# The first batch's key rotation in tiles of its own, its parts stored one by one, and a new order of steps in a two-layer adaLN kernel

## The chip, the cores and the metric

The kernel runs on one core of a Trainium2 chip. The time is that of one execution on the device in microseconds, lower is better; the median of several executions is compared. TensorE (PE, with its weight loads PEld), VectorE (DVE), ScalarE (ACT), GpSimd (POOL) and the sync engine (SP, which here issues most of the DMAs) run side by side, each through its own instructions in order, and wait for each other on semaphores.

## What is computed

Two layers, each with an attention part and a feed-forward part, both modulated per batch by rows computed from a condition (sa, ca, ga for the first part, sb, cb, gb for the second). Eight batches of 512 tokens of 128 channels. The reference, cut:

```python
mod = (_silu(L0_c) @ L0_wmod).reshape(8, 6, 1, -1)
sa, ca, ga, sb, cb, gb = ...
h = _layernorm(x) * (1 + ca) + sa
x = x + ga * attn0(h)     # 16 heads of 8, rotary q and k, softmax without scale
h = _layernorm(x) * (1 + cb) + sb
x = x + gb * ffn0(h)      # 8 experts, hidden 256, silu(h w0) * (h w1) @ wo, best two of 8
mod = (_silu(L1_c) @ L1_wmod).reshape(8, 6, 1, -1)
h = _layernorm(x) * (1 + ca) + sa
x = x + ga * attn1(h)     # v, gate = silu(n W_hidden + b); q, k from silu(n W_qk + b);
                          # softmax of q^T k / 512 over channels, summed, scales v; times gate; W_out
h = _layernorm(x) * (1 + cb) + sb
x = x + gb * ffn1(h)      # batch b goes through expert b: gelu(h w1 + b1) w2 + b2
```

The rotation turns each pair of channels of q and k by an angle that grows with the token's place: rot(t) = t cos + t2 sin, with t2 the pair exchanged and one sign changed.

## The kernel before, in words

The work of one batch passes through four stages, and batches overlap: batch b is in one stage while b+1 is in the stage before.

- **P**: layer norm and modulation, transposition, products with the weights of q, k and v, rotation, and a split of q and k (float32) into three bf16 parts each. The parts are stored to a buffer in DRAM (`parts_d`) and loaded back as stacks `qs` and `ks` of 48 rows per head, in which one bf16 product of 48 rows sums the six products of parts that make a near-float32 score.
- **A**: four groups of four heads. For each group the scores are computed once for their row maxima (`smax`: PE product, DVE reduction into negmax, 16 one-bank units per group in the first two batches, `EARLY`), the maxima are split into parts by POOL (`mparts`), turned by PE (`mT`), taken to a row by ACT and by a DMA into the stacks as rows 48 to 50; then the scores are computed again transposed with the maximum already taken off (`sexp`), exponentiated by ACT and multiplied with v (`pv`).
- **B**: the first layer's experts. Tokens are scattered by expert to DRAM, gathered in tiles, and go through w0, w1 (units) and the down product. The last batch goes through all experts densely: its down products are `ldown(e)` (L1225), its sums on DVE are at L1932.
- **C**: the second layer. `up(c)` (L1339, names xdn and w1) and `dn` (L1361) are the products of its feed-forward part, `out` (L1311) that of its attention part, `upb` (L1324) a product of a row of ones with a bias row, in the last batch only. Between `up` and `dn` DVE and ACT compute the gelu: DVE's u at L2045 takes a bank that ACT has copied and frees it for the next `up`.

**What sets the order.** On each engine the steps stand in an order given by a table of numbers, `SLOTS`: for each step (stage, name, arguments, batch) its place on each engine. `walk` issues the steps of an engine in that order. An engine does nothing out of this order, so a step that waits holds everything behind it. PE, DVE, ACT, POOL and SP have 1277, 989, 706, 530 and 667 rows of instructions in it (adjacent equal ones taken together).

**The first batch.** Its q product and then its k product go to one bank, `m1`: the k product waits until q's rotation has read it. The rotation on DVE has three steps (L1755 cos, L1757 and L1759 the two halves of sin), into tiles `rot1` and `rot2`; `first_split` (L1715) adds them to `rem`, ACT rounds `rem` to the first part (L1484), `first_split2` (L1720) takes it off, ACT rounds the second (L1488), `first_split3` (L1725) takes it off, which is the third. Rotation and split of k use the same three tiles and wait for those of q. Later batches do the split on POOL. q's three parts are stored when the third is there (three DMAs of one step), k's likewise, and the stacks are loaded in four portions of two head pairs each, 16 DMAs. The modulation rows of both layers are finished by DVE at L1689 to L1703 in one block and stored to `mod_d`, from which later rows (ga, gb, crow, cgb) are loaded.

## Time and profile before

| | |
|---|---|
| median of 3 runs | 981.61 us (981.26 to 983.02) |
| the profiled execution | 982.85 us |
| its span in the trace | 981.0 us |
| mean granted TensorE clock | 0.916 |

The runs' times are those of whole executions; the trace covers its span, 1.85 us less than the same execution took. Times within the trace are counted from the span's start.

### The profile page before, as it was taken

What the parts mean: (1) busy time and instruction counts of PE and PEld (TensorE: products, weight loads), DVE (VectorE), ACT (ScalarE), POOL (GpSimd) and SP (SyncE); (2) the same over time, 40 slices, a digit from 0 to 9 for tenths busy, and PEclk for the clock granted to TensorE, in tenths of its full rate; (3) what the DMA queues carried; (4) which work ended last, traced back from release to release, by engine and by line L of the source; (5) the groups of instructions that cost most, each with busy time, mean ns of one, the idle gap of its engine ahead of it and who ended that gap; (6) DMA issues with size and microseconds to landing.
All of it is one profiled execution on the core that took longest, in us unless ns stands there. A gap on an engine that the chain in (4) does not pass through costs nothing. (4 is left out here: it accounts for less than half of the span.)

```text
span 981.0 us, 15587 instructions
## 1 busy us (share of the span) xinstructions
PE 831.7 (85%) x4972; PEld 449.9 (46%) x4972; DVE 696.9 (71%) x1454; ACT 579.7 (59%) x923; POOL 461.6 (47%) x607
## 2 busy tenths in 40 slices
PE   4788888998789978998899989988899888799586
PEld 3222232544245515654464544634564557376353
DVE  6888786688678756788678658847877435577574
ACT  2256676575567466866686668546857864443252
POOL 0152144025458535573747367383645763663201
PEclk9558889999899979999999989989999999889688
DMA  7524344354824354446073613680156045010001
GB/s 207 164 92 99 73 99 164 86 161 130 208 52 148 122 165 92 113 123 192 25 214 95 202 28 114 182 247 17 42 179 198 25 147 180 24 39 19 1 12 38
DMA packets 97063, 110.77 MB, mean 113 GB/s; under 512 B 14191, under 2 KB 76783, under 8 KB 95616
## 3 DMA queue, kind: packets, MB, share of 16 engines
q1 hardware_dynamic: 92954, 102.06, 36.6%
q0 software_dynamic: 3584, 7.35, 2.6%
q8 instruction: 41, 0.67, 0.3%
q10 hardware_dynamic: 444, 0.36, 0.1%
q14 instruction: 40, 0.33, 0.1%
HBM read 84.06 MB, written 26.26 MB: 112 GB/s over the span
## 5 line engine op out<-in xcount | busy, mean ns | idle before, releaser
L1459 ACT ACTIVATE probs<-scores 128x1024 f32<-128x1024 f32 x256 | 262.0, 1024 | 116.0 <-PE scores L1077 84.8
L1772 DVE TENSOR_REDUCE negmax<-scores_for_max 128x2 f32<-128x1024 f32 x192 | 234.3, 1220 | 59.0 <-PE scores_for_max L1052 45.8
L1087 PE MATMUL weighted_values<-probs,vaug 128*32 128x512 f32 x1024 | 147.6, 653 | 1.1 <-ACT probs L1459 1.1
L1149 PE MATMUL expert_units<-xt,ring 128*128 128x128 f32 x840 | 122.7, 289 | 13.4 <-DVE mu L1949 5.6
L1077 PE MATMUL scores<-qs,ks 51*128 51x512 bf16 x512 | 106.0, 407 | 32.3 <-ACT probs L1459 27.9
L1149 PEld LDWEIGHTS expert_units<-xt,ring 128*128 128x128 f32 x840 | 105.2, 195 | 56.3 <-issue 47.6
L1052 PE MATMUL scores_for_max<-ks,qs 48*128 48x512 bf16 x384 | 76.8, 396 | 15.8 <-DVE negmax L1772 11.3
L2222 POOL DMA_INDIRECT xs_d<-xbn,rowpos x56 | 55.6, 994 | 50.2 <-DVE rowpos L1905 35.4
L2233 POOL DMA_INDIRECT y<-ys_d,rowpos x56 | 55.4, 989 | 37.9 <-DMA ys_d<-slot_rows 21.4
L1077 PEld LDWEIGHTS scores<-qs,ks 51*128 51x128 bf16 x512 | 25.5, 94 | 103.2 <-ACT probs L1459 64.2
L1768 DVE TENSOR_REDUCE negmax<-scores_for_max 128x1 f32<-128x512 f32 x86 | 56.4, 682 | 7.5 <-PE scores_for_max L1046 3.6
L1949 DVE SCALAR_TENSOR_TENSOR mu<-th,expert_units 128x512 f32<-128x512 f32 (+1 forms) x56 | 36.3, 648 | 31.3 <-ACT th L1514 30.2
L1204 PE MATMUL shared_ab<-ring,mu 128*128 128x128 f32 x420 | 54.7, 282 | 3.3 <-DVE mu L1959 2.0
L1204 PEld LDWEIGHTS shared_ab<-ring,mu 128*128 128x128 f32 x420 | 50.2, 194 | 13.1 <-DVE mu L1959 7.2
L2163 POOL CAST mpart<-negmax 128x16 bf16<-128x16 f32 x32 | 6.4, 201 | 102.7 <-DVE negmax L1772 64.3
L1052 PEld LDWEIGHTS scores_for_max<-ks,qs 48*128 48x128 bf16 x384 | 18.7, 94 | 74.1 <-DVE negmax L1772 47.0
L1514 ACT ACTIVATE th<-expert_units 128x512 f32<-128x512 f32 (+1 forms) x56 | 31.9, 570 | 26.0 <-PE expert_units L1149 25.8
L1959 DVE TENSOR_TENSOR mu<-mu,expert_units 128x512 f32<-128x512 f32 (+1 forms) x56 | 36.3, 648 | 15.3 <-PE expert_units L1149 14.3
L1087 PEld LDWEIGHTS weighted_values<-probs,vaug 128*32 128x32 f32 x1024 | 21.0, 111 | 41.2 <-issue 37.7
L1046 PE MATMUL scores_for_max<-ks,qs 48*128 48x512 bf16 x86 | 35.6, 483 | 3.7 <-DVE negmax L1768 3.6
L1339 PE MATMUL shared_pc<-xdn,w 128*128 128x512 f32 x56 | 33.3, 679 | 6.4 <-DVE u L2045 6.0
L1592 ACT ACTIVATE slot_rows<-shared_ab 128x512 f32<-128x512 f32 (+1 forms) x28 | 15.9, 569 | 34.1 <-PE shared_ab L1204 27.3
(325 smaller groups left out, 1666.3 us busy)
## 6 DMA issues: line engine op xcount, KB each, us to landing
ring<-in_experts SPq DMA_DIRECT2D x113, 384.0 KB, 5.2
slot_rows<-xs_d SPq DMA_DIRECT2D x7, 960.0 KB
parts_d<-parts SPq DMA_DIRECT2D x15, 384.0 KB, 2.6
qs<-parts_d SPq DMA_DIRECT2D x14, 384.0 KB
ks<-parts_d SPq DMA_DIRECT2D x14, 384.0 KB
ys_d<-slot_rows SPq DMA_DIRECT2D x21, 256.0 KB
w<-in_L_ffn_w SPq DMA_DIRECT2D x16, 256.0 KB
parts_d<-parts SPq DMA_DIRECT2D x15, 256.0 KB, 2.9
```

The costliest lines, as they stand in the source:

```text
L1052: last = nc.tensor.matmul(sm[:, 512 * m:512 * (m + 1)], qs[at, b % 2, p, t * P:(t + 1) * P], ks[at, b % 2, p, :], start=True, stop=True)
L1077: last = nc.tensor.matmul(se[:, 512 * m:512 * (m + 1)], ks[at, b % 2, p, kt * P:(kt + 1) * P], qs[at, b % 2, p, :], start=True, stop=True)
L1087: last = nc.tensor.matmul(pv[32 * j:32 * j + 32, :], vaug[:, kt, PAIRS * (j // 2) + GP * g + j % 2, :], probs[:, kt % 2, j % 2, j // 2, :] ...
L1149: last = nc.tensor.matmul(dst[:, at], ring[:, q % RING, j, first + f * P:first + (f + 1) * P], xt[:, q % 2, at], start=True, stop=True)
L1204: last = nc.tensor.matmul(m0[:, at], mu[:, (HALVES * q + f) % 4, at], ring[:, q % RING, j, 2 * HID + f * D:2 * HID + (f + 1) * D], start=( ...
L1459: nc.scalar.activation(probs[:, kt % 2, j, :, :].rearrange("p m s -> p (m s)"), se[:, :], ACT.Exp)\
L1768: V.tensor_reduce(negmax[:, g % 2, m, n:n + 1], max_unit_bank(u), AX, ALU.max, negate=True)\
L1772: V.tensor_reduce(negmax[:, g % 2, :, n], sm[:, :].rearrange("p (m s) -> p m s", m=2), AX, ALU.max, negate=True)\
L1949: V.scalar_tensor_tensor(out=mu[:, u % 4, at], in0=th[:, u % 2, at], scalar=1.0, in1=wp[:, at], op0=ALU.add, op1=ALU.mult).then_inc(sig["b ...
L1959: V.tensor_tensor(mu[:, u % 4, at], mu[:, u % 4, at], wp[:, at], ALU.mult).then_inc(sig["b_mu"], 1)
L2222: G.indirect_dma_start(xs_d[:, :], bass.IndirectOffsetOnAxis(ap=rowpos[:, b % 2, c, t:t + 1], axis=0), xbn[:, t, :], None).then_inc(sig["b ...
L2233: G.indirect_dma_start(back[c][:, t, :], None, ys_d[:, :], bass.IndirectOffsetOnAxis(ap=rowpos[:, b % 2, c, t:t + 1], axis=0))\
```

## The change

1. The first batch's k product goes to bank `m0`, and its rotation and split use the tiles `uz`, `u2` and `nt3`, which are otherwise used by the second layer; the waits of its first rotation step and its sum on q's go.
2. One of the four banks in which the modulation rows are computed is `wp` instead of `m0`. The wait for their copies moves from the first `mT` to the third maximum unit, the first that uses `wp`.
3. Each part of q and k is stored by a step of its own, after that part. The stacks of q and k are loaded by separate steps, and those of the first batch in two portions (2 head pairs, then 6) instead of four.
4. The modulation rows, the low part of W_hidden (`wh_low`) and the layer norm statistics of batch 1 wait until k's third part is written, so they stand behind the split on DVE.
5. `SLOTS` is replaced as a whole; the steps are the same except for the stores and stacks.

```diff
-    ("P", "store"): [(n,) for n in range(2)],
+    ("P", "store"): [(n, k) for n in range(2) for k in range(PARTS)],
+    ("P", "stack"): [(n,) for n in range(2)],
...
-        ("P", "stack"): dict(sp=(45, 65, 71, 83, 101, 121, 147, 177)),
-        ("P", "modst"): dict(sp=(47, 48, 49, 50, 51, 52, 53, 54)),
+        ("P", "stack"): dict(sp=(49, 50, 70, 75, 85, 86, 102, 103, 125, 126, 150, 151, 177, 180, 206, 214)),
+        ("P", "modst"): dict(sp=(51, 52, 53, 54, 55, 56, 57, 58)),
...
+M0_USES["P", "proj"] = ("p_rot", lambda n: n + 1)
...
-        mod_bank = [[m0[0:NB, 0:3 * D], pv[0:NB, 0:3 * D]], [se[0:NB, 0:3 * D], se[0:NB, 512:512 + 3 * D]]]
+        mod_bank = [[wp[0:NB, 0:3 * D], pv[0:NB, 0:3 * D]], [se[0:NB, 0:3 * D], se[0:NB, 512:512 + 3 * D]]]
...
-                    eng.wait_ge(s_rest, 64 * (GROUPS - 1))
+                    eng.wait_ge(s_rest, 64)
...
+        def proj_bank(b, n):
+            return m0 if (b, n) == (0, 1) else m1
+
+        def turned(b, n):
+
+            return (uz, u2, nt3) if (b, n) == (0, 1) else (rot1, rot2, rem)
...
-            def p_store(b, which):
-
-                after_all(sp, ("p_part2", b, which + 1))
+            def p_store(b, which, k):
+
+                after(sp, f"p_part{k}", b, which + 1)
                 stack_loaded(sp, b - 1)
-                for n in range(PARTS):
...
+                n = k if which else PARTS - 1 - k
...
+            def p_stack(b, n):
+
+                after(sp, f"p_stored{n}", b, 16 * PARTS)
+                after(sp, "a_sef", b - 2, 32)
+                dst = (qs, ks)[n]
+                for at in ((slice(0, GP), slice(GP, PAIRS)) if b == 0 else (slice(0, PAIRS),)):
+                    done = sig["p_stack"] if b else s_rest if at.start else s_first
                     for m in range(2):
...
+                        if u == 2:
+                            pe.wait_ge(s_m1, SM_COPIED)
...
-                    pe.wait_ge(s_m1, SM_COPIED)
...
                 if b == 0 and part == 0:
+                    after(dve, "p_part2", b, 2)
                     dve.wait_ge(s_colm, 3)
...
-                    after(dve, "p_part2", b, n)
-                    V.tensor_tensor(rem[:, :], rot1[:, :], rot2[:, :], ALU.add).then_inc(sig["p_sum"], 1)
+                    one, two, left = turned(b, n)
+                    V.tensor_tensor(left[:, :], one[:, :], two[:, :], ALU.add).then_inc(sig["p_sum"], 1)
...
                     dve.wait_ge(s_whh, 1)
+                    after(dve, "p_part2", b, 2)
...
+                    if (key, b) == ("p", 1):
+                        after(dve, "p_part2", 0, 2)
...
-                    after(dve, "p_sum", b, n)
-                    V.tensor_tensor(rot1[:, :], m1[:, :], cosT[:, :], ALU.mult)
+                    if (b, n) != (0, 1):
+                        after(dve, "p_sum", b, n)
+                    V.tensor_tensor(one[:, :], got[:, :], cosT[:, :], ALU.mult)
```

What the new order does is seen at three places; line numbers in rows of the new order are those of the changed kernel, where the same operation stands some 10 to 20 lines further down. The first is DVE's stretch from the end of q's rotation to the end of k's split, in the first batch. Before (`cols` are modulation columns, BN rows the statistics of batch 1, `vg` holds k's parts):

```order
L1755 TENSOR_TENSOR rot1<-shared_pc,cosT 128x512
L1725 TENSOR_TENSOR parts<-rem,parts 128x512
L1757 TENSOR_TENSOR rot2<-shared_pc,sinT 64x512
L1679 COPY cols<-scores_for_max 128x8
L1680 TENSOR_SCALAR cols<-scores_for_max 128x8
L1759 TENSOR_TENSOR rot2<-shared_pc,sinT 64x512
L1715 TENSOR_TENSOR rem<-rot1,rot2 128x512
L1737 BN_STATS stats_p<-xp 128x6 x4
L1741 BN_AGGR mv_p<-stats_p 128x2 x4
L1720 TENSOR_TENSOR rem<-rem,vg 128x512
L1725 TENSOR_TENSOR vg<-rem,vg 128x512
L1689 COPY mu<-shared_ab 8x384
```

Now, from the same q sum on:

```order
L1729 TENSOR_TENSOR rem<-rot1,rot2 128x512
L1778 TENSOR_TENSOR u2<-shared_ab,sinT 64x512
L1780 TENSOR_TENSOR u2<-shared_ab,sinT 64x512
L1735 TENSOR_TENSOR rem<-rem,parts 128x512
L1729 TENSOR_TENSOR xdn<-uz,u2 128x512
L1692 COPY cols<-scores_for_max 128x8
L1693 TENSOR_SCALAR cols<-scores_for_max 128x8
L1740 TENSOR_TENSOR parts<-rem,parts 128x512
L1735 TENSOR_TENSOR xdn<-xdn,vg 128x512
L1740 TENSOR_TENSOR vg<-xdn,vg 128x512
L1756 BN_STATS stats_p<-xp 128x6 x4
L1760 BN_AGGR mv_p<-stats_p 128x2 x4
```

k's first rotation step stands ahead of q's sum (one row above these), its second and third between q's sum and q's second step, and the statistics and W_hidden's low part (`wh_lo`, the next row) behind the last part; the block of modulation rows follows, then the first maximum.

The second place is DVE's order in group 0 of the first batch's maxima, now (before, sixteen reductions stood together, and the gate column `ga` after them; rot1 and rot2 here are batch 1's rotation):

```order
L1789 TENSOR_REDUCE negmax<-scores_for_max 128x1 x2
L1789 TENSOR_REDUCE negmax<-expert_units 128x1
L1789 TENSOR_REDUCE negmax<-scores_for_max 128x1
L1776 TENSOR_TENSOR rot1<-shared_pc,cosT 128x512
L1789 TENSOR_REDUCE negmax<-scores_for_max 128x1
L1789 TENSOR_REDUCE negmax<-expert_units 128x1
L1852 TENSOR_TENSOR ga<-wo0T,ga 128x128
L1789 TENSOR_REDUCE negmax<-scores_for_max 128x1 x2
L1778 TENSOR_TENSOR rot2<-shared_pc,sinT 64x512
L1789 TENSOR_REDUCE negmax<-expert_units 128x1
L1789 TENSOR_REDUCE negmax<-scores_for_max 128x1
L1780 TENSOR_TENSOR rot2<-shared_pc,sinT 64x512
```

Batch 1's rotation and the gate column now stand among the reductions.

The third place is PE at the end, where batch 5's up products (xdn, w1) meet the last batch's w0 and w1 products (hb, ring) and its down products (ring, mu). Before:

```order
L1005 MATMUL shared_pc<-first,xdn 128x128 x4
L1156 MATMUL scores<-hb,ring 128x512 x2
L1339 MATMUL shared_pc<-xdn,w1 128x512
L1156 MATMUL scores_for_max<-hb,ring 128x512 x2
L1339 MATMUL shared_pc<-xdn,w1 128x512 x3
L1225 MATMUL shared_ab<-ring,mu 128x128 x8
L1225 MATMUL expert_units<-ring,mu 128x128 x8
L1361 MATMUL shared_pc<-w2,kq 128x128 x8
L1156 MATMUL scores<-hb,ring 128x512 x2
```

Now:

```order
L1169 MATMUL scores<-hb,ring 128x512 x2
L1169 MATMUL scores_for_max<-hb,ring 128x512 x2
L1017 MATMUL shared_pc<-first,xdn 128x128 x4
L1352 MATMUL shared_pc<-xdn,w1 128x512 x3
L1238 MATMUL shared_ab<-ring,mu 128x128 x8
L1238 MATMUL expert_units<-ring,mu 128x128 x8
L1352 MATMUL shared_pc<-xdn,w1 128x512
L1169 MATMUL scores<-hb,ring 128x512 x2
```

The down products of experts 0 and 1 moved ahead of the last of the four up products. Further on, the two row products of batch 7 (ones, rem), which had the out product (wos, vg) between them, now both stand ahead of it:

```order
L1374 MATMUL shared_pc<-w,kq 128x128 x8
L1337 MATMUL scores_for_max<-ones,rem 128x512 x2
L1337 MATMUL scores<-ones,rem 128x512 x2
L1324 MATMUL expert_units<-wos,vg 128x128 x8
L1017 MATMUL weighted_values<-first,xdn 128x128 x4
```

Among the constants that SP loads at the start, the 14 late ones (from `bh` to `bout`, L748) now stand ahead of the tables cosT and sinT and of W_hidden (`otok`), which stood ahead of them before. On ACT the small preparations of these constants stand ahead of the copy of v (L1472) and the rounding of W_hidden behind it. On ACT and POOL the normalisation of batch 2 stands ahead of the first exponential and of group 0's `mparts`.

## Rows read from the trace of the kernel before

**Rows 1.** The page: busy time and share of the span of each engine.
```profile
PE 831.7 (85%) x4972; PEld 449.9 (46%) x4972; DVE 696.9 (71%) x1454; ACT 579.7 (59%) x923; POOL 461.6 (47%) x607
```
**Rows 2.** Windows: busy PE, PEld, DVE, ACT, POOL, granted clock, DMA share, GB/s.
```profile
40.00:60.00 20.00, 16.71 (x42) 3.31 (x41) 18.68 (x38) 6.04 (x10) 9.02 (x14) 0.50 0.44 120
60.00:80.00 20.00, 18.36 (x91) 5.25 (x89) 16.72 (x27) 13.37 (x17) 8.37 (x11) 0.75 0.44 112
840.00:860.00 20.00, 14.20 (x27) 5.65 (x28) 9.20 (x12) 10.66 (x20) 15.46 (x17) 0.79 0.10 26
860.00:880.00 20.00, 19.61 (x99) 14.42 (x98) 13.55 (x35) 8.55 (x16) 12.09 (x15) 0.87 0.18 47
```
**Rows 3.** Timeline of DVE: start, duration, operation, and the idle time before it.
```profile
16.83 0.69 DVE L1755 TENSOR_TENSOR rot<-shared_pc,cosT 128x512 f32<-128x512 f32 x1 [3.97 <-PE shared_pc L636]
...
20.35 0.69 DVE L1720 TENSOR_TENSOR rem<-rem,parts 128x512 f32<-128x512 f32 x1 [0.70 <-ACT parts L1484]
...
24.90 0.86 DVE L1737 BATCH_NORM_STATS2 stats_p<-xp 128x6 f32<-128x128 f32 x4
25.79 0.38 DVE L1741 BATCH_NORM_AGGREGATE mv_p<-stats_p 128x2 f32<-128x6 f32 x4
...
27.44 0.69 DVE L1725 TENSOR_TENSOR vg<-rem,vg 128x512 bf16<-128x512 f32 x1 [0.70 <-ACT vg L1488]
28.05 0.54 DVE L1689 COPY mu<-shared_ab 8x384 f32<-8x384 f32 x1
...
37.57 0.69 DVE L1755 TENSOR_TENSOR rot<-shared_pc,cosT 128x512 f32<-128x512 f32 x1 [1.30 <-PE shared_pc L636]
38.18 1.28 DVE L1768 TENSOR_REDUCE negmax<-scores_for_max 128x1 f32<-128x512 f32 x2
...
47.75 0.28 DVE L1831 TENSOR_TENSOR ga<-wo0T,ga 128x128 f32<-128x128 f32 x1
```
**Rows 4.** Timeline of PE: k's product, batch 1's product, the first maximum.
```profile
19.07 0.77 PE L634 MATMUL shared_pc<-hp_hi,wp_lo 128*128 128x512 f32 x1 [2.35 <-DVE rot L1759]
...
35.91 0.77 PE L634 MATMUL shared_pc<-hp_hi,wp_lo 128*128 128x512 f32 x1 [0.78 <-ACT vtok L1472]
...
37.47 0.60 PE L1046 MATMUL scores_for_max<-ks,qs 48*128 48x512 bf16 x2
```
**Rows 5.** Timeline of ACT: first normalised rows, small preparations, first exponential, batch 2's normalisation.
```profile
10.69 0.78 ACT L1428 ACTIVATE xp<-shared_pc,cols 128x512 f32<-128x512 f32 x1 [1.14 <-DVE cols L1680]
...
15.90 0.21 ACT L1404 ACTIVATE bhh<-bh 128x4 f32<-128x4 f32 x1 [0.94 <-DMA bout<-in_L_attn_b_out]
...
54.19 1.02 ACT L1459 ACTIVATE probs<-scores 128x1024 f32<-128x1024 f32 x1 [0.33 <-PE scores L1077]
...
57.15 1.65 ACT L1443 ACTIVATE xp<-xp,shift_p,rstd_p 128x128 f32<-128x128 f32 x4 [0.21 <-POOL shift_p L2119]
```
**Rows 6.** Timeline of SP's queue: when each DMA is issued, and how long issuing took.
```profile
12.30 0.47 SPq L748 DMA_DIRECT2D bout<-in_L_attn_b_out  x1
...
39.73 0.46 SPq L803 DMA_DIRECT2D mod_d<-mu  x1
...
43.88 0.43 SPq L851 DMA_DIRECT2D ga<-mod_d  x1
```
**Rows 7.** Timeline of PE: batch 5's last up products, the last batch's down products.
```profile
855.21 2.07 PE L1339 MATMUL shared_pc<-xdn,w 128*128 128x512 f32 x2 [2.32 <-DVE u L2045]
859.34 2.07 PE L1339 MATMUL shared_pc<-xdn,w 128*128 128x512 f32 x2 [2.05 <-DVE u L2045]
861.20 3.62 PE L1225 MATMUL shared_ab<-ring,mu 128*128 128x128 f32 x16
```
**Rows 8.** Timeline of all engines near the end: out product, second row product, DVE's next step.
```profile
957.51 2.02 PE L1311 MATMUL expert_units<-wos,vg 128*128 128x128 f32 x16 [0.17 <-issue]
959.46 1.98 PE L1324 MATMUL scores<-ones,rem 1*128 1x512 f32 x4
...
960.66 0.69 DVE L2036 TENSOR_TENSOR x<-expert_units,hc 128x512 f32<-128x512 f32 x1 [2.92 <-DMA out<-x]
```

More of the change, by code:

```diff
@@ L88 @@
 SLOTS = {
[L89 to L93 removed]
+        ("B", "ldown"): dict(pe=(1, 2, 3, 4, 5, 6, 7, 8, 9, 10, 11, 12, 13, 14, 15, 18, 31, 32, 33, 34, 35, 36, 37,
@@ L253 @@
-        ("C", "mod"): dict(dve=(42, 97, 98, 99, 100, 101, 102, 955), pool=(103, 144, 184, 220, 255, 295, 326, 327)),
-        ("B", "weights"): dict(dve=(106, 107, 115, 116, 117, 118, 119, 911)),
-        ("C", "keep"): dict(dve=(108, 109, 110, 111, 112, 113, 114, 958), pool=(109, 147, 186, 225, 258, 297, 329,
+        ("P", "hT"): dict(act=(18, 41, 47, 113, 168, 232, 334, 427)),
+        ("P", "small"): dict(act=(19, 20, 21, 22, 23, 24, 25, 26)),
+        ("P", "whhi"): dict(act=(28, 30, 31, 32, 33, 34, 35, 36)),
@@ L308 @@
-        ("C", "rstd3"): dict(pool=(134, 174, 210, 252, 289, 305, 339, 344)),
-        ("P", "load"): dict(sp=(1, 31, 46, 72, 84, 102, 122, 149)),
-        ("P", "raw"): dict(sp=(2, 4, 5, 6, 14, 15, 16, 17)),
-        ("P", "rope"): dict(sp=(3, 7, 18, 19, 20, 21, 22, 23)),
-        ("P", "late"): dict(sp=(8, 9, 12, 13, 26, 27, 28, 29)),
-        ("B", "blank"): dict(sp=(10, 11, 24, 25, 33, 40, 41, 42)),
-        ("P", "second"): dict(sp=(30, 32, 34, 35, 36, 37, 38, 39)),
-        ("P", "store"): dict(sp=(43, 44, 62, 64, 67, 69, 79, 81, 92, 97, 111, 113, 140, 144, 168, 174)),
@@ L323 @@
[L323 to L328 removed]
+        ("B", "x2"): dict(pool=(99, 139, 180, 213, 251, 290, 323, 324)),
@@ new lines @@
+        ("C", "rstd"): dict(pool=(101, 141, 183, 216, 253, 292, 325, 338)),
+        ("C", "rstd2"): dict(pool=(106, 145, 186, 222, 257, 296, 328, 340)),
+        ("C", "lo"): dict(pool=(110, 148, 188, 228, 261, 298, 331, 332)),
+        ("C", "rstd3"): dict(pool=(136, 175, 217, 252, 291, 309, 339, 344)),
+        ("P", "late"): dict(sp=(1, 2, 3, 4, 5, 6, 7, 8)),
+        ("P", "rope"): dict(sp=(9, 12, 13, 14, 15, 16, 17, 18)),
+        ("P", "load"): dict(sp=(10, 42, 59, 87, 104, 127, 152, 179)),
@@ new lines @@
+        ("B", "blank"): dict(sp=(11, 19, 20, 21, 30, 39, 40, 41)),
+        ("P", "raw"): dict(sp=(22, 23, 24, 25, 28, 29, 31, 32)),
+        ("P", "second"): dict(sp=(26, 27, 33, 34, 35, 36, 37, 38)),
+        ("P", "store"): dict(sp=(43, 44, 45, 46, 47, 48, 66, 67, 69, 71, 72, 73, 76, 77, 78, 80, 81, 82, 92, 95, 96,
+        98, 99, 100, 112, 113, 114, 118, 120, 121, 132, 133, 134, 139, 140, 142, 164, 165, 168, 173, 175, 178, 200,
+        202, 204, 207, 209, 210)),
+        ("P", "stack"): dict(sp=(49, 50, 70, 75, 85, 86, 102, 103, 125, 126, 150, 151, 177, 180, 206, 214)),
@@ L364, with in_bank @@
 IN_OTHER_BANKS = ("xT", "qk", "hid", "sim", "out", "xT3", "up", "dn")
+def in_bank(uses, stage, step, b, *args):
+    if (stage, step) == ("P", "proj") and (uses is M0_USES) != (b == 0 and args[0] == 1):
+        return False
+    return (stage, step) in uses and not elsewhere(stage, step, b, *args)
 def elsewhere(stage, step, b, *args):
@@ L612, in bank_waits @@
         def bank_waits(uses, b, stage, step, *args):
-            order = [u for u in order_of("pe") if u[:2] in uses and not elsewhere(u[0], u[1], u[3], *u[2])]
+            order = [u for u in order_of("pe") if in_bank(uses, u[0], u[1], u[3], *u[2])]
             at = order.index((stage, step, args, b))
@@ L1749, in rot @@
             def rot(b, n, k):
+                got, (one, two, _) = proj_bank(b, n), turned(b, n)
                 if k == 0:
```

354 lines of the change are left out of this document (170 added, 184 removed), and 116 rows, old and new, of the table SLOTS.

## Prediction

> **What bounds the kernel now.** I read the page's busy times first, then 20 us windows, then the lines of each engine in the windows where the changed order differs most: the first 60 us and the last 140. Over the span PE is busy 85% and DVE 71%, with no engine full [rows 1], so the mean says little; the stages have different limits. From 40 to 60 us DVE is busy 18.68 of 20 us while PE, at half its clock (0.50 granted, the 1.2 GHz level), has 16.71: here the row maxima on DVE set the pace. From 60 to 80 us DVE still has 16.72. From 840 to 860 PE is down to 14.20 and from 860 to 880 it is at 19.61 [rows 2], so a wait of PE just before 860 is paid in full, and one in the middle of a DVE queue with slack is not. The start is serial: nothing can begin before the first batch's queries and keys are rotated, split, stored and loaded back, and the chain runs through DVE.
>
> **Start, DVE.** In the kernel before, the first rotation starts at 16.83 and the last part of k is written at 28.13 (27.44 + 0.69), 11.30 us [rows 3]. Two things in it go. The statistics of batch 1 (0.86 + 0.38 = 1.24) move behind k's split. And of the two waits of 0.70 for ScalarE's rounding [rows 3] one is covered, since the key's rotation, in tiles of its own, now stands between q's subtraction and q's second one; the last one stays, as k's last two steps are adjacent. So 11.30 - 1.24 - 0.70 = 9.36, and k is done near 26.2. PE's wait of 2.35 for q's third rotation step [rows 4] goes as well; what it delayed is the product that DVE reads in this same stretch, so it is no second saving.
>
> What now follows k's split is the statistics (1.24), the low part of W_hidden (one full-size operation, 0.69 like the rotation's first) and the modulation rows. The rows take from 28.05 to 36.27, that is 37.57 less the idle 1.30, or 8.22 us [rows 3]. The first maximum is then ready to start at 26.2 + 1.24 + 0.69 + 8.22 = 36.35 instead of 38.18. Of the 1.83 gained 0.69 is only order, as one rotation step of batch 1 stood ahead of it and now stands behind: **-1.1**. The stack load must have arrived by then. It is issued after the last part's store; the parts of q and the first two of k have been stored by then one by one, so it starts earlier than before by about the 1.9 that k is earlier, and the load before had landed by 37.47 at the latest [rows 4]; 35.6 is before 36.35. The key's first portion stands behind the second portion of the queries, however, which is the risk of this step.
>
> The Trainium skill, DMA: Bandwidth & Descriptors, section Queues, rings and completion order, says that descriptors on one ring are consumed in order: the key's two head pairs would be read only after six pairs of the query. No row here shows such a pair of loads. The same page's section Anatomy of one DMA gives 436 GB/s for the variable part; the 590 KB ahead (two halves of 48 rows of 3072 two-byte values) would by that add some 1.4 us, an estimate, and the first maximum would start near 37.0 and not 36.35.
>
> **Start, other engines.** Putting off W_hidden's low part takes 0.69 from ahead of the column copies; ScalarE waited 1.14 for these at 10.69 [rows 5], so its normalised rows can come up to 0.69 sooner. Against that ScalarE's small preparations now stand ahead of the copy of v, and the first of them waited for a load issued at 12.30 and seen at 15.90, 3.6 us after its issue [rows 5, 6]. Three loads now stand behind it instead of ahead, three issues of 0.47 [rows 6], so it lands near 14.5. This part is between -0.7 and +1.5; the copied bank is needed again only by batch 1, and I take **0**.
>
> **Group 0, DVE.** The gate column (ga) moves from 47.75 [rows 3], after sixteen maxima, to after the first six. Its load waits for the store of the modulation rows, which cannot leave before these are done. Before, store at 39.73 and load at 43.88 were 4.15 apart, with two issues between that now stand elsewhere, so about 3.2 net [rows 6]. Now: store 36.4, load 39.6, and DVE comes to it after six maxima (0.60 apart: sixteen from 38.18 to 47.75), a rotation step (0.7) and 0.45 of waiting for PE, which puts the batch 1 product (1.56 from 35.91 to 37.47, [rows 4]) between maxima: 41.1. That leaves 1.5 us for a landing that took at most 3.9 before (43.88 to 47.75). The stall is 0 to 2.4; I take 0.4, near the lower end, as 3.9 is only the time after which it was used without a wait. All ten maxima of the group, and what PE does with them, are queued behind it. With the 0.45: **+0.85**.
>
> The group's sixteen maxima now have four rotation steps (2.8) and the statistics of batch 2 (1.24) among them. The last ends near 36.35 + 16 x 0.60 + 4.0 + 0.2 + 0.85 = 51.0 instead of 47.75, and the first exponential, which followed 6.4 us later (54.19, [rows 5]), comes near 57.5: 3.3 late. What was put ahead is not lost: ScalarE's normalisation of batch 2, which stood between exponentials (1.65 at 57.15, [rows 5]), and GpSimd's gain for w2, which stood behind the group's maxima, are done by then. DVE sets the pace here and does the same operations in another order, so I take **0**; the whole 3.3 is a rival below.
>
> **Middle.** Every engine's steps are rearranged, but the steps ahead of each batch's last maximum and last exponential differ by no more than about eight for batch 1 and four for the later ones, as the orders show. No step is added. **0**, between -2 and +2.
>
> **Tail.** PE waits 2.32 us at 855.21 and 2.05 at 859.34 for the two last up products of batch 5, both times for DVE's u, and only at 861.20 starts the down products of the last batch's experts 0 and 1 [rows 7]. These now stand before the last up. They start after the third up, near 857.3, 3.9 earlier; the last up is still to be done, 1.86 from 859.34 to 861.20, or half of that if it then runs at the higher clock (0.79 was granted over 840 to 860 and 0.87 over the next 20 us, [rows 2]). So 2.05 to 3.0 earlier; I take **-2.4**. Since PE is busy 19.61 of the 20 us that follow [rows 2], this should pass on.
>
> **End.** Both row products of batch 7 now stand ahead of its output product, so that one comes 1.98 later [rows 8]. But DVE's next step, at 960.66, had waited 2.92 and not for PE: for the output store of the buffer that it writes [rows 8]. The product started at 957.51 and ran 2.02, ending 1.13 before that. So about 0.9 shows, less what the store is earlier because of the work above: between 0 and +1.98, I take **+0.5**.
>
> **Sum:** -1.1 + 0 + 0.85 + 0 - 2.4 + 0.5 = -2.15. The profiled execution took 982.85, 1.85 more than its span of 981.0 and 1.24 above the median of the runs (981.61). 982.85 - 2.15 = 980.70, and at the median 979.46, say 979.5. About 0.2%, 1.96 us, is what a measurement of this kernel can tell from no change: faster means under 979.65, slower over 983.57.
>
> **Rivals.**
> - *The late first exponential is not made up* (0.28). For it: group 0's maxima are interleaved with batch 1's and 2's work, and PE, ScalarE and GpSimd wait in order behind the first exponentials; in 40 to 60 ScalarE was busy only 6.04 us [rows 2], so it cannot be the reserve from which the time comes back unless exponentials later run back to back. Against it: DVE, not ScalarE, is full there. Price: -2.15 + 3.3 = +1.15, 982.8; with the gate stall at its upper end, 2.0 more, 984.8. It decides against the change from 4.1 us lost upward, so with the stall from 0.8 over what I took.
> - *The tail's gain is given back* (0.16). The last batch's down products need weights, and DVE must turn them into y; if PE then waits for u all the same, -2.15 + 2.4 = +0.25: 981.9. For it: DVE's u is late because of a chain through ScalarE, which the order does not shorten.
> - *TensorE gets its full clock earlier* (0.14). Between 40 and 60 us the granted clock was 0.50, though PE was busy 16.71 us, and 0.75 in the next window [rows 2]. The new order packs products of batch 1 between the maxima. If PE goes over to the 2.4 GHz level earlier, DVE no longer waits for it and its idle in 40 to 80, 1.32 + 3.28 = 4.6, is the most that comes back; I take three quarters, 3.5, so 976.0. The Trainium skill, TensorE: Matmul & The Clock Gate, Part 1, says that the throttled state is the default and that sustained activity releases it. The trace does not agree in this window, 16.71 busy of 20 at 0.50, so the page gives no more than this chance.
> - *The change doesn't do what it says*: the key's portion comes behind the queries' second portion so late that the first maximum is no earlier than 38.18. Then the -1.1 goes, 980.6; it is inside the forecast's own spread.
>
> **Numbers.** The forecast (0.42) has its own range 977.5 to 981.0; 0.29 of it lies under 979.65 and 0.13 in the band. The clock's 0.14 is faster too: 0.43. The same: 0.13, of the tail's rival 0.14, of the late exponential's 0.08: 0.35. Slower: 0.20 of the late exponential and 0.02 of the tail: 0.22. The 8-in-10 range reaches from 976 to 985, which takes in the clock's and the stall's upper ends and the middle's 2 us.
>
> **What would show it.** Right: k's last part near 26.2 on DVE, the first maximum near 36.4, no wait of PE over 1 us before the last up of batch 5, and the end after the last down products 2 us earlier. Wrong: a wait of DVE over 2 us at ga; a first maximum that waits for the stack; ScalarE's exponentials behind those of before by 3 us still at the end of batch 0; a wait of 2 us that turns up at the last batch's units instead; a granted clock that differs over whole stages.

## The result and the profile after

The changed kernel takes 1003.07 us (median of 3 runs, 996.33 to 1009.54) beside 981.61: a ratio of 1.0211, 95% interval 1.0152 to 1.0271. It is about 21 us slower; the prediction said 979.5. Its profiled execution took 1009.54 us, the slowest of the three, with a span of 1006.8. The page's busy times:

```profile
PE 833.3 (83%) x4972; PEld 454.1 (45%) x4972; DVE 696.7 (69%) x1454; ACT 580.5 (58%) x923; POOL 461.1 (46%) x607
```

They differ from those of [rows 1] by under 5 us on every engine, with the same number of instructions. The span grew by 25.8 us all the same: the time is idle time, and the question is who waits, where, and for what.

**The start came as forecast.** DVE (start, duration, operation, idle before it), beside [rows 3]:

```profile
17.42 0.69 DVE L1776 TENSOR_TENSOR rot<-shared_pc,cosT 128x512 f32<-128x512 f32 x1 [4.55 <-PE shared_pc L647]
...
25.75 0.69 DVE L1740 TENSOR_TENSOR vg<-xdn,vg 128x512 bf16<-128x512 f32 x1 [0.70 <-ACT vg L1501]
26.48 0.87 DVE L1756 BATCH_NORM_STATS2 stats_p<-xp 128x6 f32<-128x128 f32 x4
...
36.40 1.29 DVE L1789 TENSOR_REDUCE negmax<-scores_for_max 128x1 f32<-128x512 f32 x2
38.94 0.69 DVE L1789 TENSOR_REDUCE negmax<-expert_units 128x1 f32<-128x512 f32 x1 [1.25 <-PE scores_for_max L1060]
...
40.80 0.69 DVE L1776 TENSOR_TENSOR rot<-shared_pc,cosT 128x512 f32<-128x512 f32 x1 [0.58 <-PE shared_pc L647]
...
42.60 0.28 DVE L1852 TENSOR_TENSOR ga<-wo0T,ga 128x128 f32<-128x128 f32 x1
```

PE, the first maximum's product and what follows it, beside [rows 4]:

```profile
35.76 0.61 PE L1060 MATMUL scores_for_max<-ks,qs 48*128 48x512 bf16 x2 [2.76 <-DMA ks<-parts_d]
36.29 2.07 PE L1045 MATMUL shared_pc<-wv,xp 128*128 128x128 f32 x8
```

ACT, the first exponential of batch 0 and that of batch 1, beside the 54.19 of [rows 5]:

```profile
58.27 1.02 ACT L1472 ACTIVATE probs<-scores 128x1024 f32<-128x1024 f32 x1 [0.57 <-PE scores L1090]
...
113.20 1.02 ACT L1472 ACTIVATE probs<-scores 128x1024 f32<-128x1024 f32 x1 [1.66 <-PE weighted_values L1100]
```

The first exponential is 4.1 late; batch 1's is 6.9 early, since it stands at 120.06 before. So at 113 us the new kernel leads. The windows say how (as in [rows 2]; the last two stretches are longer):

```profile
40.00:60.00 20.00, 13.72 (x36) 3.40 (x35) 18.02 (x36) 5.55 (x11) 10.17 (x15) 0.50 0.52 131
60.00:80.00 20.00, 17.18 (x94) 4.74 (x92) 17.62 (x30) 13.87 (x17) 8.02 (x10) 0.88 0.56 131
60.00:120.00 60.00, 51.22 (x323) 14.79 (x324) 51.61 (x88) 43.00 (x52) 14.01 (x28) 0.96 0.41 93
755.00:773.00 18.00, 9.65 (x55) 4.63 (x58) 6.66 (x14) 5.29 (x10) 12.86 (x13) 0.86 0.82 256
```

From 60 to 120 us the clock was 0.96; in the kernel before it was 0.80 there. The last row is the other side. In 18 us PE is busy 9.65, DVE 6.66, ACT 5.29, and POOL, which runs 13 indirect DMAs, is with 12.86 the busiest. The lead is gone by batch 3 (first exponential 2.3 late), and the lag grows to 4.0, 7.5, 12.7 and 13.5 us for batches 4 to 7; the last exponential is 20.8 late (825.86 for 805.05) and the end 25.8. **Most of the loss arises between batch 1's first exponential and the last one, in the middle, which I had put at nothing;** another 5 us lie behind it.

**What the 18 us look like.** PE, ACT, DVE and POOL, each from its timeline:

```profile
762.85 0.39 PE L1090 MATMUL scores<-qs,ks 51*128 51x512 bf16 x2
763.30 0.39 PE L1066 MATMUL scores_for_max<-ks,qs 48*128 48x512 bf16 x2
...
772.14 0.61 PE L1090 MATMUL scores<-qs,ks 51*128 51x512 bf16 x2 [7.35 <-issue]
```
```profile
771.06 1.02 ACT L1472 ACTIVATE probs<-scores 128x1024 f32<-128x1024 f32 x1 [7.36 <-remote]
```
```profile
773.16 1.23 DVE L1793 TENSOR_REDUCE negmax<-scores_for_max 128x2 f32<-128x1024 f32 x1 [7.68 <-remote]
```
```profile
754.99 1.03 POOL L2243 DMA_INDIRECT xs_d<-xbn,rowpos  x1 [0.49 <-issue]
...
760.48 0.96 POOL L2243 DMA_INDIRECT xs_d<-xbn,rowpos  x1 [0.30 <-issue]
761.74 1.01 POOL L2254 DMA_INDIRECT y<-ys_d,rowpos  x1 [0.31 <-issue]
...
770.58 0.94 POOL L2254 DMA_INDIRECT y<-ys_d,rowpos  x1 [0.31 <-issue]
```

PE had finished the scores by 763.24 and the maximum's scores by 763.69. ACT takes up the first at 771.06 and DVE the second at 773.16, 7.8 and 9.5 us after the product's end. Both rows name "remote": the semaphore that ended the wait rose, but no row that raises it had ended shortly before. In the traces this semaphore is one of PE's in every such wait of ACT and DVE, 14 before and 21 now; here its rises are recorded at 771.04 and 773.13, 0.02 and 0.03 us before the readers start. So PE's signal came late, as far as the ends of PE's rows, which are modelled, can be trusted. PE, which needs the readers' results, stands idle too. Such starts lie in the runs of indirect DMAs: the scatter (L2243) and the gather (L2254) of the expert layer's rows, eight of each for each of seven batches. In the kernel before, the scatter and the gather of this place were apart, with other work between:

```profile
745.57 0.96 POOL L2222 DMA_INDIRECT xs_d<-xbn,rowpos  x1 [0.30 <-issue]
752.21 1.00 POOL L2233 DMA_INDIRECT y<-ys_d,rowpos  x1 [5.68 <-DMA ys_d<-slot_rows]
...
756.03 0.94 POOL L2233 DMA_INDIRECT y<-ys_d,rowpos  x1 [0.30 <-issue]
...
760.41 0.98 POOL L2233 DMA_INDIRECT y<-ys_d,rowpos  x1 [0.46 <-issue]
```

There, from 741.4 to 771.4, PE is busy 27.14 of 30 us at a clock of 1.00. The groups of ACT's exponentials and DVE's two-tile maxima, before and after (count | busy, mean ns | idle before it and for whom):

```profile
L1459 ACT ACTIVATE probs<-scores 128x1024 f32<-128x1024 f32 x256 | 262.0, 1024 | 116.0 <-PE scores L1077 84.8 <-PE weighted_values L1087 12.3 <-remote 10.1
L1772 DVE TENSOR_REDUCE negmax<-scores_for_max 128x2 f32<-128x1024 f32 x192 | 234.3, 1220 | 59.0 <-PE scores_for_max L1052 45.8 <-remote 5.4 <-issue 4.0
```
```profile
L1472 ACT ACTIVATE probs<-scores 128x1024 f32<-128x1024 f32 x256 | 262.0, 1023 | 139.8 <-PE scores L1090 78.2 <-remote 39.1 <-PE weighted_values L1100 11.9
L1793 DVE TENSOR_REDUCE negmax<-scores_for_max 128x2 f32<-128x1024 f32 x192 | 234.3, 1220 | 106.2 <-PE scores_for_max L1066 68.5 <-remote 31.6 <-POOL mpart L2190 3.7
```

In these groups remote idle rose from 10.1 to 39.1 us on ACT and from 5.4 to 31.6 on DVE. Over all instructions the rise is smaller, from 25.2 to 44.2 and from 13.1 to 34.3, since the kernel before has such waits on other steps too. Often both wait in the same microseconds: the time in which at least one of them does is 27.0 us before and 51.7 now, 24.7 more, close to the 25.8 by which the spans differ. It is time waited and not all of it lost: from batch 1's first exponential to batch 6's the changed kernel loses 19.6 us, and these waits grow by 8.3 there. The other idle of ACT's exponentials fell; that of DVE's maxima rose by 21 us, nearly all of it for PE (45.8 to 68.5).

The length of a run of indirect DMAs (rows less than 0.7 us apart) is what such waits go with. In the kernel before, none of the 25 runs of one to five has one in it or just behind it, and all seven of six to eight have, the longest of each from 1.9 to 5.0 us. In the changed kernel one of 14 runs of up to four has, and all ten of five or more. The two longest, 12 at 662 to 677 us and 13 at 755 to 771, are the only ones in which gathers follow scatters at once; their waits reach 7.4 and 7.7 us, and 21.6 of the 51.7 us lie there. The load of the DMA engines does not decide it: in the kernel before, five in a row had none at a DMA share of 0.97 (142.9 to 149.0), and six had 1.9 us at 0.18 (354.6 to 362.0).

**The tail and the end.** PE at batch 5's last up products, beside [rows 7]:

```profile
876.37 1.42 PE L1352 MATMUL shared_pc<-xdn,w 128*128 128x512 f32 x2 [2.15 <-DVE u L2066]
880.00 2.08 PE L1352 MATMUL shared_pc<-xdn,w 128*128 128x512 f32 x2 [2.21 <-DVE u L2066]
881.86 2.92 PE L1238 MATMUL shared_ab<-ring,mu 128*128 128x128 f32 x16
...
886.41 1.02 PE L1352 MATMUL shared_pc<-xdn,w 128*128 128x512 f32 x2
```

The wait ahead of the last up is gone, as forecast. The third up starts 24.8 late (880.00 for 855.21), 4.0 more than the last exponential, and the first row product of the end 22.0 late (977.36 for 955.37): of what was behind, 2.8 us came back between them. The end, beside [rows 8]:

```profile
977.36 1.98 PE L1337 MATMUL scores_for_max<-ones,rem 1*128 1x512 f32 x4
...
979.44 3.73 PE L1337 MATMUL scores<-ones,rem 1*128 1x512 f32 x4
...
983.10 3.56 PE L1324 MATMUL expert_units<-wos,vg 128*128 128x128 f32 x16
...
986.70 0.69 DVE L2057 TENSOR_TENSOR x<-expert_units,hc 128x512 f32<-128x512 f32 x1 [7.16 <-PE expert_units L1324]
```

DVE's step comes 9.34 us after the first row product, for 5.30 before (955.37 to 960.66). It waits for PE now, and PE is slow: granted clock 0.66 from 977 to 987, 1.00 before from 955 to 961.

### The profile page after: what moved, and what is told of

It reads as the page before. It is cut to its first block and busy times, and to the rows that moved or that the text cites. A ratio compares the mean times of both kernels' runs of the same rounds, so it can differ in the third digit from the quotient of the medians.

```text
span 1006.8 us, 15611 instructions
## 1 busy us (share of the span) xinstructions
PE 833.3 (83%) x4972; PEld 454.1 (45%) x4972; DVE 696.7 (69%) x1454; ACT 580.5 (58%) x923; POOL 461.1 (46%) x607
## 3 DMA queue, kind: packets, MB, share of 16 engines
q0 software_dynamic: 3584, 7.35, 2.5%
## 5 line engine op out<-in xcount | busy, mean ns | idle before, releaser
L1472 ACT ACTIVATE probs<-scores 128x1024 f32<-128x1024 f32 x256 | 262.0, 1023 | 139.8 <-PE scores L1090 78.2
L1793 DVE TENSOR_REDUCE negmax<-scores_for_max 128x2 f32<-128x1024 f32 x192 | 234.3, 1220 | 106.2 <-PE scores_for_max L1066 68.5
L2243 POOL DMA_INDIRECT xs_d<-xbn,rowpos x56 | 55.6, 992 | 38.4 <-DVE rowpos L1926 23.0
L2254 POOL DMA_INDIRECT y<-ys_d,rowpos x56 | 54.8, 979 | 40.0 <-DMA ys_d<-slot_rows 23.7
L1217 PE MATMUL shared_ab<-ring,mu 128*128 128x128 f32 x420 | 58.3, 284 | 1.7 <-ACT xt L1594 1.5
L1527 ACT ACTIVATE th<-expert_units 128x512 f32<-128x512 f32 (+1 forms) x56 | 31.9, 570 | 39.1 <-PE expert_units L1162 38.4
L746 POOL TENSOR_TENSOR kq<-qz,gam 128x512 f32<-128x512 f32 x14 | 17.8, 1272 | 40.1 <-PE shared_pc L1374 28.9
```

Source lines behind the costliest of these rows:

```text
L1217: last = nc.tensor.matmul(m0[:, at], mu[:, (HALVES * q + f) % 4, at], ring[:, q % RING, j, 2 * HID + f * D:2 * HID + (f + 1) * D], start=( ...
L1472: nc.scalar.activation(probs[:, kt % 2, j, :, :].rearrange("p m s -> p (m s)"), se[:, :], ACT.Exp)\
L1793: V.tensor_reduce(negmax[:, g % 2, :, n], sm[:, :].rearrange("p (m s) -> p m s", m=2), AX, ALU.max, negate=True)\
L2243: G.indirect_dma_start(xs_d[:, :], bass.IndirectOffsetOnAxis(ap=rowpos[:, b % 2, c, t:t + 1], axis=0), xbn[:, t, :], None).then_inc(sig["b ...
L2254: G.indirect_dma_start(back[c][:, t, :], None, ys_d[:, :], bass.IndirectOffsetOnAxis(ap=rowpos[:, b % 2, c, t:t + 1], axis=0))\
```

## Experiments

Two theories stood against each other. The first: the middle's new order brings scatter and gather together, and what TensorE finishes in such a run of indirect DMAs reaches DVE and ACT late. The rival: the late start is not made up, or the new order of steps is worse by itself. Executions of either order spread (the kernel before, on the chips of these runs, from 973 to 991, medians 980 to 983), so every ratio is to runs of before on the same chip.

**Where in the program is it lost?** The changed code, with the new order up to the first exponential of batch 0, 3, 5 or 7 and the old order behind it. Only the table of slots is edited; one line of it, as in `new_to_b5`, where the last batch stands again where it stood before:

```diff
-        ("P", "xT"): dict(pe=(86, 137, 152, 280, 389, 510, 691, 858)),
+        ("P", "xT"): dict(pe=(86, 137, 152, 280, 389, 510, 691, 929)),
```

> The changed code, with the new order on every engine up to batch 0's first exponential and the order of before from there on (stores and stacks as the changed code needs them). In the trace of the changed kernel the first exponentials of batch 1 come 6.9 us earlier than before (113.2 against 120.1), and the delay grows only later. Theory 'later order': the start, with its own bank, single stores and late modulation rows, costs nothing or gains; 976 to 983. Rival 'start' (the late first exponential at 58.3 against 54.2 is carried through, and the split stores disturb every batch): 990 or more.

> The new order up to batch 3's first exponential, then the old. In the traces the first exponential of batch 3 stands 2.3 us behind. Theory 'later order, spread over the batches': 982 to 986. Rival 'start': 990 or more. Rival 'the last batches alone': as new_start within 2 us.

> The new order up to batch 5's first exponential, then the old. The first exponential of batch 5 stands 7.5 us behind in the traces. Theory 'later order, spread': 986 to 991. Rival 'the last batches alone': 978 to 983. Rival 'start': 990 or more.

> The new order up to batch 7's first exponential, then the old (tail of before). That exponential stands 13.5 us behind in the traces, and the end 25. Theory 'later order, spread': 992 to 997, and the rest of the loss lies in the tail. Rival 'the tail alone' (last batch's expert layer): 978 to 984. Rival 'chance': the executions of the changed kernel lie 13 us apart, so the loss could be of no place in particular; then all four lie near 990 with a wide spread.

Measured: `new_start` 985.89, ratio 1.0034 (1.0000 to 1.0067); `new_to_b3` 983.98, 1.0032 (0.9997 to 1.0067); `new_to_b5` 990.28, 1.0091 (1.0049 to 1.0132); `new_to_b7` 998.23, 1.0163 (1.0110 to 1.0215). The start costs 0 to 7 us, the new order of batches 0 to 2 adds nothing that shows, the loss grows over batches 3 to 6, and the 0.5% that is left of the 2.1% is within these intervals. The run of 13 indirect DMAs shown above lies behind batch 7's first exponential; `new_to_b7` has the one of 12 and not this one. In `new_start` the first exponential of batch 1 stands at 124.93, 4.9 behind: without the new order behind it, the late start is not made up.

**Take the indirect DMAs away.** In both kernels each scatter and gather becomes a plain DMA of as many rows, still from POOL; the rows then don't go to their experts' places. The scatter's edit (the gather's is alike):

```diff
-                G.indirect_dma_start(xs_d[:, :], bass.IndirectOffsetOnAxis(ap=rowpos[:, b % 2, c, t:t + 1], axis=0),
-                                     xbn[:, t, :], None).then_inc(sig["b_sent"], 16)
+                at = (c * NT + t) * P
+                G.dma_start(xs_d[at:at + P, :], xbn[:, t, :]).then_inc(sig["b_sent"], 16)
```

> The kernel before, with the scatters and gathers of the expert layer as plain DMAs of the same bytes from GpSimd (tokens go to rows in their own order and not to their expert's, so the result is not the reference's). Theory 'runs of indirect DMAs': while GpSimd issues several of them in a row, DVE and ACT get TensorE's results microseconds late; without them both kernels gain, this one 5 to 15 us: 966 to 976. Rival 'order of the other steps': the indirect DMAs are hidden; within 3 us of before, 978 to 984.

> The changed kernel with the same plain DMAs (the same part of the computation is left out). Theory 'runs of indirect DMAs': its runs are longer (13 in a row at 755 to 771 us, 12 at 662 to 677), so it gains more, 20 us or more, and stands within 6 us of the kernel before with plain DMAs: 968 to 981. Rival 'order of the other steps': the distance of some 20 us stays: 995 to 1005.

Measured: 946.41, ratio 0.9648 (0.9583 to 0.9713), and 950.21, 0.9674 (0.9613 to 0.9735). The kernel before gains 35 us by it, the changed kernel 53: the distance falls from 21 us to 3.8 by medians, 1.0027 by ratios, which these intervals can't tell from nothing. Both times lie well under what I expected: the old order, too, pays for its indirect DMAs. A plain DMA is also shorter on POOL than an indirect one (last section), so this edit alone does not tell the lateness from the time on POOL. The same groups in the changed kernel with plain DMAs:

```profile
L1472 ACT ACTIVATE probs<-scores 128x1024 f32<-128x1024 f32 x256 | 261.9, 1023 | 100.2 <-PE scores L1090 86.8 <-PE weighted_values L1100 12.7
L1793 DVE TENSOR_REDUCE negmax<-scores_for_max 128x2 f32<-128x1024 f32 x192 | 234.4, 1221 | 63.1 <-PE scores_for_max L1066 60.1 <-POOL mpart L2190 1.4 <-POOL mrem L2186 0.9
```

No remote is left on either engine, in this kernel or in `before_plain`.

**One indirect DMA at a time.** They stay, but each waits until the one before has landed:

```diff
+                if 2 * t + c:
+                    after(pool, "b_sent", b, 16 * (2 * t + c))
                 G.indirect_dma_start(xs_d[:, :], bass.IndirectOffsetOnAxis(ap=rowpos[:, b % 2, c, t:t + 1], axis=0),
```

> The kernel before with the same waits. Theory 'runs', by number under way: 972 to 982, since its late starts of 1 to 3 us go too, and GpSimd's longer runs cost a part. By the rival: 982 to 992, the later gathers delay the second layer.

> The changed kernel, where each scatter and gather waits until the one before it in its batch has landed. GpSimd needs longer for them, but never has two of them under way. Theory 'runs', if it is the number of descriptors under way that holds up signals: 985 to 997, and the late starts of DVE and ACT behind TensorE at 661 to 680 and 755 to 771 are gone. If it is their making on GpSimd alone, or by the rival, later expert layers only add: 1003 to 1015.

Measured: 1143.08, ratio 1.1649 (1.1561 to 1.1736), and 1156.47, 1.1767 (1.1688 to 1.1846). The times expected of my theory were wrong, and the two orders are still 1.0% apart. Remote idle is gone from both groups of both kernels, as it says, but I had left out the price of waiting. POOL in `before_paced`:

```profile
157.04 0.96 POOL L2224 DMA_INDIRECT xs_d<-xbn,rowpos  x1 [2.50 <-DMA xs_d<-xbn,rowpos]
160.05 0.96 POOL L2224 DMA_INDIRECT xs_d<-xbn,rowpos  x1 [2.05 <-DMA xs_d<-xbn,rowpos]
163.06 0.96 POOL L2224 DMA_INDIRECT xs_d<-xbn,rowpos  x1 [2.05 <-DMA xs_d<-xbn,rowpos]
```

One comes every 3.0 us, where it came every 1.26: POOL's row of 0.96 is not the transfer. The Trainium skill, Perfetto Trace Analysis, section DMA Instruction — SWDGE (GPSIMD), says that the profile's end of such an instruction is when its descriptors are made, not when the data has moved. The trace agrees: 2.05 us of landing behind each row.

**A break after four, and two under way.** Milder forms: a wait only ahead of the fifth of the eight (`_c4`), and two semaphores in place of one, so that each waits for the one before the last (`_two`).

```diff
+                if 2 * t + c == 4:
+                    after(pool, "b_sent", b, 64)
```
```diff
+                j, k = (2 * t + c) % PACE, (2 * t + c) // PACE
+                if k:
+                    after(pool, f"b_sent{j}", b, 16 * k)
...
-                                     xbn[:, t, :], None).then_inc(sig["b_sent"], 16)
+                                     xbn[:, t, :], None).then_inc(sig[f"b_sent{j}"], 16)
```

> The changed kernel, where the fifth scatter and the fifth gather of a batch wait until the four before have landed: the runs of 8 are broken into two of 4, at the cost of one landing, some 2 us, each (14 in all). Theory 'long runs': the late starts sit at the ends of long runs, so most go: 985 to 1003. Rival 'shorter on GpSimd': the waits only add, up to 28 us: 1005 to 1030.

> The kernel before with the same break after four. Its runs are already broken in some batches by the order (3, 2, 3 or 4, 4). Theory: 975 to 995, the distance to the changed kernel with the same break under 12. Rival: 985 to 1010 and the distance stays near 20.

> The changed kernel with at most two scatters, and at most two gathers, under way in a batch (each waits for the one before the last; two semaphores in place of one, so nothing else differs). With a break after four the distance between the two kernels had fallen from 21 to some 3 us, late starts of DVE and ACT behind TensorE from 70 to 26 us. Theory 'several indirect DMAs under way make the signals late': hardly any late starts; 1.5 to 2 us per indirect DMA instead of 1.25, 112 of them, of which a part shows: 985 to 1010. Rival 'the break moved other work, and the lateness is only where it shows': late starts as in the changed kernel, 1000 to 1020.

> The kernel before with the same limit of two. Theory: hardly any late starts, 975 to 1000, and within 6 us of the changed kernel with this limit. Rival: the distance of 20 us stays. If it comes under 978 it beats both kernels.

Measured: `after_c4` 993.27, 1.0145 (1.0091 to 1.0198); `before_c4` 990.74, 1.0111 (1.0069 to 1.0153); `after_two` 1018.44, 1.0392 (1.0341 to 1.0443); `before_two` 1009.39, 1.0303 (1.0251 to 1.0354). With the break the distance between the orders is 0.34%, with two under way 0.9%, instead of 2.1%. Remote idle of the two groups falls to 9.2 and 10.3 in `after_c4` and to nothing in the other three. Over all instructions of ACT and DVE together, `after_c4` keeps 24.7 us of 78.5 and `before_c4` 3.3 of 38.3; 18.0 of the 24.7 lie at the two places where scatter and gather meet, in runs of eight there. POOL's rows stay at 0.97 to 0.99 us in `after_c4`, and waits were only added, so the distance between the orders does not need a shorter time on POOL to go. Both times of `_two`, and its distance of 9 us, are over what my theory gave. The waits put time on the path in place of the remote idle, in `after_two`:

```profile
L2252 POOL DMA_INDIRECT xs_d<-xbn,rowpos x56 | 55.2, 985 | 73.0 <-DMA xs_d<-xbn,rowpos 37.1 <-DVE rowpos L1932 23.0 <-issue 12.9
L2266 POOL DMA_INDIRECT y<-ys_d,rowpos x56 | 54.2, 967 | 87.7 <-DMA y<-ys_d,rowpos 55.5 <-DMA ys_d<-slot_rows 19.3 <-issue 12.6
```

POOL waits 37.1 + 55.5 = 92.6 us for landings here and 37.9 + 34.5 = 72.4 in `before_two`, which may be why the two orders still differ; that is not shown. So a break is no remedy; it only shows what the lateness hangs on.

**The rest, without indirect DMAs.** The parts of the change one behind the other, all with plain DMAs on one chip: the old kernel again, new start, new order to batch 7, the whole.

```diff
-        ('P', 'xT'): dict(pe=(86, 137, 152, 278, 389, 512, 671, 929)),
+        ('P', 'xT'): dict(pe=(86, 137, 152, 280, 389, 510, 691, 858)),
```

(from `start_plain` to `b7_plain`, one line of the table)

> The kernel before with plain DMAs (tokens at rows of their own order, as in before_plain), again beside the three that follow, so that the four compare on one chip without the indirect DMAs' spread: 944 to 949.

> As new_start (changed code, new order up to batch 0's first exponential, old order behind it), with plain DMAs. Theory 'the start gives nothing lasting': the first exponential 4 to 5 us later than before and partly made up, 0 to +4 against b_plain2. By the prediction's terms for the start and group 0 (-1.1 and +0.85): -0.3 against b_plain2. By its slower rival (the late exponential is not made up): +3 or more.

> As new_to_b7 (new order up to batch 7's first exponential, the tail old), with plain DMAs: what the middle costs without indirect DMAs. Theory: the distance left in the plain pair, about 4 us, comes from the middle: +2 to +8 against b_plain2. By the prediction's 0 for the middle: within 2 of start_plain.

> The changed kernel with plain DMAs, again. Against b7_plain it differs by the tail alone: by the prediction's terms (-2.4 for the down products ahead of the last up, +0.5 for the row products) -1.9; by its rival (the gain is given back) +0.5; if the new tail is worse, +2 to +6. Against b_plain2: +2 to +6.

Measured: 948.76, 948.98, 953.79 and 949.61, ratios 0.9636 (0.9589 to 0.9683), 0.9662 (0.9617 to 0.9707), 0.9706 (0.9657 to 0.9754) and 0.9664 (0.9622 to 0.9707). Step by step +0.2, +4.8 and -4.2 us, in all +0.9 (by ratio 0.28%, 2.7 us). Each time has an interval of some 4.5 us to either side, so no single step can be told from nothing. The traces, in the same order, add where: the first exponential of batch 1 stands at 120.97, 123.92, 112.65 and 113.25, that of batch 7 at 657.56, 662.88, 662.12 and 658.26. With the new middle there is a lead of 8 us at batch 1, and at batch 7 a lag of 1 to 5. So in these executions the new middle loses 8 to 13 us between them even without indirect DMAs, and the lead hides most of it.

**The tail by itself.** The kernel before, with its order to the first exponential of batch 7 and the new order behind it, with indirect DMAs and with plain ones:

```diff
-        ("C", "upb"): dict(pe=(20, 21, 22, 23, 24, 25, 26, 27, 28, 29, 30, 31, 32, 33, 1364, 1367)),
+        ('C', 'upb'): dict(pe=(20, 21, 22, 23, 24, 25, 26, 27, 28, 29, 30, 31, 32, 33, 1364, 1365)),
```

> The kernel before, code and order, up to batch 7's first exponential, and the changed kernel's order behind it: the tail alone, with the indirect DMAs of batches 5 and 6 in it. With plain DMAs the new tail was worth some 4 us (953.8 to 949.6). Theory 'the prediction's tail term holds, the loss is in the middle's indirect DMAs': 975 to 979 and faster than before, the best of all. Rival 'the new tail, too, puts indirect DMAs together' (in the changed kernel 13 in a row at 755 to 771 us, before batch 7's last maxima): 981 to 990.

> The same with plain DMAs (tokens at rows of their own order). Theory: 3 to 5 us under the kernel before with plain DMAs (948.8 and 946.4 so far), 943 to 946. Rival (the tail's gain in a_plain2 against b7_plain came only from what the new middle had left over): 947 to 950.

Measured: 996.61, ratio 1.0160 (1.0114 to 1.0206), and 954.14, 0.9735 (0.9686 to 0.9785). No gain: 14 us slower than before, and 5.4 slower than the old order with plain DMAs (954.14 against 948.76, from another chip; 1.0% by ratios). Both are over the ranges of my theory and of its rival. The rival's cause is there: `tail_only` has 13 indirect DMAs in one run at 747 to 764 us, gathers behind scatters, as the changed kernel has. But in its profile 5.6 of 15.9 us are lost ahead of batch 7's first exponential, where the order is the old one. The -4.2 above is thus at least in part only what fits behind the new middle. Two orders joined at one point also fit badly there, `new_to_b7` perhaps as well, and these runs don't separate that from the tail's own worth. No version beat the kernel before with the routing left in.

## Why the prediction was wrong

**The step that failed: "Middle. 0, between -2 and +2".** It counted that no step is added and that the steps ahead of each batch's last maximum and exponential differ by no more than eight or four, and did not ask which steps come to lie beside each other. The middle lost 20.8 - 4.1 = 16.7 us between the first exponential and the last in the profiles: 10.9 gained up to batch 1's first, 27.7 lost from there. Taking the indirect DMAs away brings the whole distance from 21 to between 1 and 4 us by medians, so most of the 21 hangs on them: that is shown. That it goes by how many of them follow each other at once is supported by the count of runs and by `_c4`, `_two` and `_paced`; the 1% between the orders in the last two is not explained by it. The step could have been priced: the kernel before has 27.0 us of such waits, all at runs of six to eight, and POOL's timeline beside the new order shows scatter and gather moving together.

How much it is in an execution is partly chance: `new_to_b7` and the changed kernel have one order up to batch 7's first exponential, and in their profiles, the fastest of four executions and the slowest of three, it stands at 697.5 and 707.1. The runs of the changed kernel spread by 13 us.

**Start.** k done at 26.44 for 26.2 (the stretch took 9.02 for 9.36 and began 0.59 later), the first maximum at 36.40 for 36.35, no stall at `ga` for 0.4; DVE's two waits for PE are 1.25 + 0.58 = 1.83 for 0.45, since PE puts batch 1's v product (2.07 at 36.29) between two maxima. That makes the group +1.8 instead of +0.85, and the first exponential 58.27 for 57.5. The key's portion, which I called the risk, held PE for 2.76 us and let it start at 35.76, and DVE did not wait. By the Trainium skill, DMA: Bandwidth & Descriptors, section Queues, rings and completion order, the estimate had been 37.0; the trace does not bear out the delay.

**The late first exponential.** I argued that DVE does the same operations and makes it up. In `new_start` it is not: 5.4 late at batch 0 (59.56), 4.9 at batch 1, 5.9 at the end. With the new order behind it, it is, by more than asked. So the rival at 0.28 holds for the start alone, at 0 to 7 us measured for 3.3, and not for this kernel.

**TensorE's clock earlier.** This came, 0.88 for 0.75 from 60 to 80 and 0.96 for 0.80 from 60 to 120, and it goes with the 6.9 us of lead at batch 1. The rival took a gain there to last to the end; it was gone by batch 3.

**Tail.** The mechanism was right, the wait of 2 us is gone, and 2.8 us came back behind it for 2.4 forecast. That this shortens the kernel is not shown: `tail_only` and `tail_plain` lose. That the gain is given back, a rival at 0.16, is nearer to what they show. The last rival, that the first maximum is no earlier than 38.18, is out with 36.40.

**End.** The sign and place were right; the size was +4.0 (9.34 for 5.30) where I took +0.5, at most 1.98. The missing part is the lower clock, at which the second row product took 3.73 for 1.98 and the output product 3.56 for 2.02.

**What stays open.** Why PE's semaphores rise late is not in the traces, nor whether the signal alone is held up or PE itself, since the ends of its rows are modelled. The record of semaphores has gaps there, too: 400 of the 896 rises of the scatters' semaphore in the changed kernel, all 896 in `after_plain`. Nor is it settled why the new middle loses its lead without indirect DMAs.

## What to carry to other kernels

When a change only reorders, list for each queue which steps come to lie next to each other, and look first at those that were already late for no visible reason: idle put down to "remote" is a warning against bringing more of its cause together. Here the length of a run of indirect DMAs was the thing to count. An order that leaves DMA runs of two neighbouring stages apart can be worth more than all the waits that a reordering removes. Before arguing over 2 us, learn how far executions of one kernel differ, and cut a change along the program rather than by its parts when the loss grows slowly.

## What the runs showed of the hardware

- Where POOL issued five or more indirect DMAs in a row, 1.26 us apart, ACT or DVE had a remote wait in 17 of 18 runs of the two kernels, and started up to 9.5 us after the end of the product that it read; in runs of up to four, in 1 of 38. With at most two under way, or with plain DMAs of as many rows, no remote idle was left in the two groups above.
- A plain DMA of as many rows occupied POOL for 0.56 us and an indirect one for 0.99 (scatters, 56 of each, in the changed kernel):

```profile
L2244 POOL DMA_DIRECT2D xs_d<-xbn x56 | 30.9, 557 | 23.9 <-DVE rowpos L1926 23.0 <-issue 0.8
```
```profile
L2243 POOL DMA_INDIRECT xs_d<-xbn,rowpos x56 | 55.6, 992 | 38.4 <-DVE rowpos L1926 23.0 <-issue 15.3
```

- An indirect DMA that is waited for costs 3.0 us from one to the next; with such a wait ahead of 98 of the 112, the two kernels took 162 and 153 us longer.
- PE was slower behind such a wait: the same pair of score products takes 0.39 us at 762.85, where the granted clock was 1.00 (755 to 763), and 0.61 at 772.14 after the 7.35 us of idle, where it was 0.50 (772 to 778).
